# Routed experts of a decoder layer: blocks of two 64-row pieces in place of blocks of 128 rows

## The reference, cut to what matters

```python
x = x + attn(layernorm(x)); x = x + xattn(layernorm(x), ctx, ctx)
h0 = layernorm(x)                                   # 1024 tokens of 256
shared = (silu_and_mul(h0 @ shared_gate_up_w.T) @ shared_down_w.T) * sigmoid(h0 @ sgate_w.T)
routing_weights = softmax(h0 @ gate_w.T)            # 16 experts
topk_w, topk_ids = top_k(routing_weights, 4)
for e in range(16):                                 # w13[e]: 352 x 256, w2[e]: 256 x 176
    coef = sum(where(topk_ids == e, topk_w, 0.0), axis=-1)
    acc = acc + (silu_and_mul(h0 @ w13[e].T) @ w2[e].T) * coef[:, None]
out = x + shared + acc
```

## Time and profile before

| | us |
|---|---|
| median of 3 runs | 385.86 |
| lowest and highest run | 384.45 and 387.84 |
| the profiled execution, its own time | 389.97 |
| its span, from first to last instruction | 388.1 |

### The profile page before, as it was taken

One profiled execution on the slowest core, in us unless ns is written; L12 is line 12 of the kernel. 1 busy time (PEld: TensorE's weight loads), 2 busy tenths in 40 slices (PEclk: granted clock), 3 DMA queues, 4 the chain that ended last, 5 costly groups with the idle time before them and its releaser, 6 DMA issues.

```text
span 388.1 us, 7610 instructions
## 1 busy us (share of the span) xinstructions
PE 346.5 (89%) x2118; PEld 246.7 (64%) x2134; DVE 236.1 (61%) x730; ACT 182.4 (47%) x538; POOL 145.6 (38%) x179
## 2 busy tenths in 40 slices
PE   6988799999999998777869939999999999999883
PEld 2455376777666865556748626777777777778652
DVE  3296669898898499653445524444444444443995
ACT  1264579898878586735406213333333333332220
POOL 5491314362544140757157400333333333332000
PEclk9899799999999699885898979999999999999996
DMA  7997866778595814312112153677777777754901
GB/s 227 334 301 279 371 193 199 225 232 280 156 346 159 266 45 151 96 44 84 43 56 96 66 145 89 212 215 206 208 221 215 204 219 200 231 175 152 371 15 54
DMA packets 47365, 71.60 MB, mean 184 GB/s; under 512 B 5619, under 2 KB 35332, under 8 KB 46692
## 3 DMA queue, kind: packets, MB, share of 16 engines
q1 hardware_dynamic: 42692, 59.79, 50.2%
q0 software_dynamic: 3792, 10.49, 7.1%
q10 hardware_dynamic: 848, 0.92, 1.0%
HBM read 39.07 MB, written 32.12 MB: 183 GB/s over the span
## 4 chain that ended last, share of the span: by engine, by line
PE 32%; issue 25%; POOL 16%; DVE 14%; ACT 7%; DMA 3%; SPq 1%; POOLq 0%; DVEq 0%; ACTq 0%
POOL y_picks L605 11%; PE bank L1417 10%; ACT probs L641 6%; PE bank L1339 4%; PE bank L1295 3%; PE bank L1331 3%; DVE neg_max L881 2%; DVE x L1255 2%; POOL x_slots L551 2%; PE bank L1326 2%; PE bank L1387 2%; PE bank L1360 2%; PE bank L1400 1%; DVE probs_t L887 1%; PE bank L1368 1%
## 5 line engine op out<-in xcount | busy, mean ns | idle before, releaser
L605 POOL DMA_INDIRECT y_picks<-yb,ids x47 | 45.1, 960 | 85.9 <-DVE yb L1227 85.2
L641 ACT ACTIVATE probs<-bank,neg_max 128x128 f32<-128x128 f32 x256 | 70.1, 417 | 7.3 <-DVE neg_max L881 7.3
L1670 PE MATMUL bank<-w,xbt 128*128 x188 | 65.7, 474 | 0.6 <-ACT xbt L772 0.6
L1220 DVE TENSOR_TENSOR hb<-sg,bank 128x176 f32<-128x176 f32 x47 | 15.9, 339 | 60.2 <-ACT sg L780 53.4
L780 ACT ACTIVATE sg<-bank 128x176 f32<-128x176 f32 x47 | 14.9, 317 | 76.4 <-issue 56.8
L1690 PE MATMUL bank<-w,hbt 128*128 128x256 f32 x188 | 48.2, 380 | 0.0
L1670 PEld LDWEIGHTS bank<-w,xbt 128*128 128x128 f32 x188 | 32.9, 194 | 18.4 <-issue 2.5
L881 DVE TENSOR_REDUCE neg_max<-bank 128x4 f32<-128x512 f32 x64 | 41.4, 681 | 5.0 <-PE bank L1331 4.9
L1339 PE MATMUL bank<-ident,probs 128*128 128x128 f32 x256 | 40.1, 289 | 4.5 <-ACT probs L641 4.0
L551 POOL DMA_INDIRECT x_slots<-x,slots x32 | 32.2, 1006 | 28.0 <-DVE slots L1010 19.6
L1339 PEld LDWEIGHTS bank<-ident,probs 128*128 128x128 f32 x256 | 30.4, 147 | 11.3 <-ACT probs L641 10.9
(11 more groups left out here) (172 smaller groups left out, 668.5 us busy)
## 6 DMA issues: line engine op xcount, KB each, us to landing
x_slots<-zero_b SPq DMA_DIRECT2D x16, 1056.0 KB, 8.8
w<-w_in_dram SPq DMA_DIRECT2D x47, 256.0 KB
xb<-x_slots SPq DMA_DIRECT2D x47, 132.0 KB
w<-w_in_dram SPq DMA_DIRECT2D x4, 1408.0 KB, 11.6
yg<-y_picks SPq DMA_DIRECT2D x8, 512.0 KB, 7.0
ktc<-keys_d SPq DMA_DIRECT2D x16, 192.0 KB, 3.2
sw_raw<-shared_in_dram SPq DMA_DIRECT2D x6, 384.0 KB, 3.3
keys_d<-ctxt_h SPq DMA_DIRECT2D x4, 512.0 KB, 6.4
```

Of the source, the lines that this page charges most:

```text
L605: pool.indirect_dma_start(y_picks[:, :], bass.IndirectOffsetOnAxis(ids[:, n:n + 1], 0), yb[:, n % RB, :], None).then_inc(yb_placed[n % RB] ...
L641: ins = act.activation(probs[:, g, j, :], ps_s[g][:, 128 * j:128 * j + 128], ACT.Exp, bias=neg_max[:, g, j:j + 1])
L1670: ins = pe.matmul(ps_gu[n % 2][:, 0:GU], xbt[:, n % 2, k, :], w13[:, bass.ds(e, 1), k, :].rearrange("p e n -> p (e n)"), start=k == 0, sto ...
```

## The change

The blocks become pairs of 64-row pieces, the even and the odd piece each with its own expert: NBLK is 40 (79 pieces at most). The even piece has stationary columns and output rows 0 to 63, the odd one 64 to 127, in `block_up` and `block_down`. The even piece's weights are read by a register in place, `w13` and `w2`, of which now all 16 experts are in SBUF; the odd piece's up weights are copied by ScalarE into `w13_odd` (two buffers, `copy_up`), and its down weights are loaded by SyncE into `w2_odd` (a ring of RW = 3). The rows of a block no longer stand together, so GpSimd loads them by an indirect DMA with 128 row numbers (`gather_rows`). The table is made for both pieces.

```diff
-NBLK = (B * T * TOPK + NE * 127) // 128
+ROWS = 64
+NBLK = -(-((B * T * TOPK + NE * (ROWS - 1)) // ROWS) // 2)
+RW = 3
 RB = 4
...
+NEXP = WORDS * PACK
...
+        w13_odd = place("w13_odd", [128, 2, KC, GU])
+        w2_odd = place("w2_odd", [128, RW, KC, D])
...
-        w2 = place("w2", [128, RB, KC, D])
+        w2 = place("w2", [128, NE, KC, D])
...
             def load_down(n):
 
-                if n >= RB:
-                    sp.wait_ge(yb_psum, n - RB + 1)
+                if n >= RW:
+                    sp.wait_ge(yb_psum, n - RW + 1)
                 e = sp.value_load(table[0:1, n:n + 1], min_val=0, max_val=NE - 1)
...
+                sp.dma_start(w2_odd[:, n % RW, :, :].rearrange("p k d -> p (k d)"),
+                             w2_in[:, bass.ds(e, 1), :, :].rearrange("p e k d -> p (e k d)")).then_inc(w2_odd_loaded[n % RW], 16)
 
             sp.wait_ge(x3_ready, B)
+            for i in range(4):
+                es = slice(4 * i, 4 * i + 4)
+                sp.dma_start(w2[:, es, :, :], w2_in[:, es, :, :]).then_inc(w2_loaded, 16)
             sp.wait_ge(table_ready, 3)
-            for n in range(RB - 1):
+            for n in range(NBLK):
                 load_down(n)
-            sp.wait_ge(scattered, 16 * TOPK * B)
-            for n in range(RB + 1):
-                load_rows(n)
...
+            def gather_rows(n):
+
+                if n >= RB:
+                    pool.wait_ge(xbt_psum, n - RB + 1)
+                    pool.wait_ge(ids_ready, n - RB + 1)
+                pool.indirect_dma_start(xb[:, n % RB, :], None, x_slots[:, :],
+                                        bass.IndirectOffsetOnAxis(rows[:, n:n + 1], 0)).then_inc(xb_loaded[n % RB], 16)
+
+            pool.wait_ge(x3_ready, B)
+            pool.wait_ge(table_ready, 1)
+            pool.wait_ge(scattered, 16 * TOPK * B)
+            for n in range(RB):
+                gather_rows(n)
             for n in range(NBLK):
-                place_rows(n)
+                if n + RB < NBLK:
+                    gather_rows(n + RB)
+                if n:
+                    place_rows(n - 1)
+            place_rows(NBLK - 1)
...
+            act.wait_ge(table_ready, 2)
+            packed = [act.value_load(words[0:1, WORDS + i:WORDS + i + 1], min_val=0, max_val=NE ** PACK - 1) for i in range(WORDS)]
+            number = act.alloc_register("expert_odd")
+
+            def copy_up(n):
+
+                act.reg_alu(number, packed[n // PACK], 4 * (n % PACK), ALU.logical_shift_right)
+                act.reg_alu(number, number, NE - 1, ALU.bitwise_and)
+                e = act.snap(number, min_val=0, max_val=NE - 1)
+                if n >= 2:
+                    act.wait_ge(gu_psum, n - 1)
+                act.activation(w13_odd[:, n % 2, :, :], w13[:, bass.ds(e, 1), :, :].rearrange("p e k n -> p (e k) n"), ACT.Copy
+                               ).then_inc(w13_odd_ready, 1)
+
+            act.wait_ge(w13_loaded, 64)
+            act.wait_ge(x2_ready, B)
+            copy_up(0)
+            copy_up(1)
             take_rows_t(0)
             take_rows_t(1)
             block_gate(0)
+            copy_up(2)
             for n in range(NBLK):
                 if n + 1 < NBLK:
                     block_gate(n + 1)
                 take_hidden_t(n)
                 if n + 2 < NBLK:
                     take_rows_t(n + 2)
+                if n + 3 < NBLK:
+                    copy_up(n + 3)
...
             def block_table():
 
-                pe.wait_ge(after_ready, 1)
...
+                pe.wait_ge(after_ready, 2)
+                for part in range(2):
+                    at = TABLE_AT + NBLK * part
+                    for i in range(2):
+                        pe.matmul(ps_t[ROWS * i:ROWS * i + ROWS, at:at + NBLK], upto[:, NE:NE + ROWS],
+                                  after[:, part, i:2 * NBLK:2], start=True, stop=True)
+                at = TABLE_AT + 2 * NBLK
+                for i in range(2):
+                    ins = pe.matmul(ps_t[0:1, at + NEXP * i:at + NEXP * i + NEXP], upto[:, NE:NE + 1], after[:, 0, i::2],
+                                    start=True, stop=True)
+                ins.then_inc(table_psum, 1)
...
-                e = experts[n]
+                pe.wait_ge(w13_odd_ready, n + 1)
                 for k in range(KC):
-                    ins = pe.matmul(ps_gu[n % 2][:, 0:GU], xbt[:, n % 2, k, :],
-                                    w13[:, bass.ds(e, 1), k, :].rearrange("p e n -> p (e n)"), start=k == 0, stop=k == KC - 1)
+                    pe.matmul(ps_gu[n % 2][0:ROWS, 0:GU], xbt[:, n % 2, k, 0:ROWS],
+                              w13[:, bass.ds(experts[n], 1), k, :].rearrange("p e n -> p (e n)"), start=k == 0, stop=k == KC - 1)
+                    ins = pe.matmul(ps_gu[n % 2][ROWS:128, 0:GU], xbt[:, n % 2, k, ROWS:128], w13_odd[:, n % 2, k, :],
+                                    start=k == 0, stop=k == KC - 1)
...
                 for k in range(KC):
-                    ins = pe.matmul(ps_yb[n % 2][:, 0:D], hbt[:, n % 2, k, :], w2[:, n % RB, k, :], start=k == 0, stop=k == KC - 1)
+                    pe.matmul(ps_yb[n % 2][0:ROWS, 0:D], hbt[:, n % 2, k, 0:ROWS],
+                              w2[:, bass.ds(experts[n], 1), k, :].rearrange("p e n -> p (e n)"), start=k == 0, stop=k == KC - 1)
+                    ins = pe.matmul(ps_yb[n % 2][ROWS:128, 0:D], hbt[:, n % 2, k, ROWS:128], w2_odd[:, n % RW, k, :],
+                                    start=k == 0, stop=k == KC - 1)
```

More of the change, by code:

```diff
@@ L93, in decoder_layer @@
         tri = place("tri", [128, 2, 128], BF16)
-        upto = place("upto", [NE, NE + 128 + NBLK])
-        dump = place("dump", [128, NBLK])
+        upto = place("upto", [NE, NE + 128 + 2 * NEXP])
+        dump = place("dump", [128, 2 * NBLK + 1])
+        rows = place("rows", [128, NBLK], U32)
+        rows_f = place("rows_f", [128, NBLK])
         of_block = place("of_block", [128, NBLK])
@@ L131, in decoder_layer @@
         counts_i = place("counts_i", [NE, 2], I32)
-        after = place("after", [NE, NBLK])
-        table = place("table", [1, 2 * NBLK], I32)
-        words = place("words", [1, WORDS], I32)
+        after = place("after", [NE, 2, 2 * NEXP])
+        table = place("table", [1, NBLK], I32)
+        words = place("words", [1, 2 * WORDS], I32)
         ex = place("ex", [128, B, NE])
@@ L148, in decoder_layer @@
         cursor[0] = shared_at
[L149 to L153 removed]
+        packs = place("packs", [1, 2 * NEXP])
+        packed_f = place("packed_f", [1, 2 * NEXP])
+        words_f = place("words_f", [1, 2 * WORDS])
         cursor[0] = after_shared
@@ L353, in decoder_layer @@
         xb_loaded = [sem(f"xb_loaded{r}") for r in range(RB)]
-        w2_loaded = [sem(f"w2_loaded{r}") for r in range(RB)]
+        w2_loaded = sem("w2_loaded")
+        w2_odd_loaded = [sem(f"w2_odd_loaded{r}") for r in range(RW)]
+        w13_odd_ready = sem("w13_odd_ready")
         yb_placed = [sem(f"yb_placed{r}") for r in range(RB)]
@@ L1699, in _ @@
             pe.wait_ge(rows_added, HB)
+            pe.wait_ge(w2_loaded, 64)
             for n in range(NBLK):
```

70 lines of the change are left out of this document (25 added, 45 removed).

## The result

The changed kernel takes 375.73 us (median of 4 executions, 374.28 to 380.67) where the kernel before, run beside it, takes 386.85 us (384.45 to 388.37). The ratio is 0.9706, 95% interval 0.9631 to 0.978: faster. Ratios here leave out executions that are over 1.5% above the fastest of their kernel; medians don't. The profiled execution of the changed kernel took 375.47 us, with a span of 373.6, so it is like its median; the profiled one of before, 389.97, lay 3 us above the 386.85 here and 4 us above the 385.86 that the prediction started from.

A forecast was written before the change was run, and what follows sets the result against it. TensorE was taken to bound the block loop: 47 blocks at 2.50 us (117.5) become 40 at 2.80 (112.0), plus 0.4 at the start, 5.1 less. From the median 385.86 that gives 380.8 us, 8-in-10 range 375 to 394.

The forecast's parts named there:

- halves abreast at the price of one: Block loop on TensorE: two 64-column halves stream side by side, down 0.87 and up 1.19 us per block as now.
- rival 2: Halves don't overlap fully: period 3.32 us, time 402, chance 0.05; no overlap at all: 4.86 a block, 463, chance 0.02.
- the two switches together: TensorE, each block: changing between halves and full width adds 0.30 us (0.28 to 0.35), making the period 2.80.
- ScalarE's copy: Block loop: copying the odd piece's up weights on ScalarE takes 0.79 us, with 0.8 us cover, nothing on the path.
- rival 3: The path over xbt or the sequencer sets the period, 2.87 to 3.0 us: time 386, chance 0.15.
- rival 4: Switches hide, for instance behind waiting loads: period 2.50 to 2.60 us, time 371, chance 0.06.
- GpSimd's 2 x 1.27 = 2.54: Block loop: GpSimd's gather and scatter together take 2.54 of the 2.80 us period, fitting by 0.26.
- rival 1: GpSimd becomes the bound if a gather's span passes 1.22 us; at 1.6 the time is 396, chance 0.10.
- The forecast charged 0.4: Start of the block loop: word reads, table matmuls and slower first switches make 0.1 us; 0.4 taken because ScalarE stands close.
- The table's matmuls: Ahead of the loop on TensorE: two small matmuls taking 0.51 us become six with some two more switches, 0.5 us more.
- its like would take 384.9: Whole kernel: the profiled execution of 389.97 us less the 5.1 us forecast gain.
- the median of the runs is 4.1 lower: Whole kernel: median before is 385.86 us, 4.1 under the profiled execution; minus 5.1 gives 380.8.

The follow-up runs named there:

- run 6: Changed kernel with blocks taken two at a time on TensorE (two blocks' up passes, all their transposes, two blocks' down passes): 374.38 us, ratio 0.9755 to the kernel before.
- run 2: Changed kernel with up and down matmuls at full width, the even piece's expert for all 128 rows, odd experts left out: 370.07 us, ratio 0.9629.
- before with zeros at 42 us: Kernel before with six products of zeros on TensorE in the attention loop's wait near 42 us: 383.51 us, ratio 0.9996.
- run 4: Changed kernel with TensorE and ScalarE reading only the first word of experts ahead of the loop, the others in it: 380.17 us, ratio 0.986.
- changed with zeros at 42 us: Changed kernel with six products of zeros on TensorE in the attention loop's wait near 42 us: 378.31 us, ratio 0.9789.
- warm start: Changed kernel with products of zeros on TensorE behind each word it reads and behind the first transposes, ahead of the blocks: 379.09 us, ratio 0.9726.
- pairs and warm start: Changed kernel with blocks taken two at a time on TensorE and products of zeros ahead of the blocks: 378.92 us, ratio 0.9821.
- pairs, four buffers: Changed kernel with blocks taken two at a time and four rather than three buffers for the odd pieces' down weights: 376.73 us, ratio 0.977.
- all four: Changed kernel with blocks two at a time, four odd down-weight buffers, products of zeros ahead of the blocks and near 42 us: 376.06 us, ratio 0.9737.

## Why the prediction was right, and where it was off

*The forecast's own steps.* What it said of the loop held to one or two hundredths: halves abreast at the price of one (both forms of rival 2 fall, 402 and 463), period 2.785 for 2.80, the two switches together 0.285 for 0.30, 40 blocks at 2.785 = 111.4 for 112.0. That is 6.1 us less than 117.5 where 5.5 was worked out; from first up pass to last place the gain is 6.4. ScalarE's copy took 0.791 for 0.79; no path over `xbt` appeared (rival 3), TensorE was busy 20.00 of 20.00 us; the switches did not hide (rival 4), and run 6 takes one pair of them out and finds 0.30 us in the period. GpSimd's 2 x 1.27 = 2.54 left the 0.25 us that was forecast (rival 1), and run 2 shows the point from which it decides, 2.55 us a block.
By the Trainium skill, TensorEngine Tiling (Array Packing), Key Properties, a change of tiling mode drains TensorE. The trace agrees: 1.28 us for up passes that take 1.19 where no change follows, and 0.30 us less for one pair of switches less in run 6. By the Trainium skill, TensorE: Matmul & The Clock Gate, Part 3, The mechanism, matmuls are strictly in order in start and end. In this trace the odd half's first pass (281.77) starts ahead of the even half's second pass (282.06), which belongs to the instruction issued before it. So for fp32 matmuls in two passes the starts are not in order pass by pass; of the ends the trace can't tell, since they are modelled.

*The start of the loop.* The forecast charged 0.4. From the last scatter to the first up pass it was 10.7 us in three profiles of the changed kernel's start, and 9.7, 11.4 and 11.4 in three of the kernel before. The kernel with 47 blocks, whose eight words are as many as the kernel before reads, took 11.4 too. From the last x3 addition it is 34.4 to 34.5 with eight words (before, before with zeros at 42 us, 47 blocks) and 33.7 with seven (the changed kernel's three), and the clock's loss between explains at most 0.3 of that. So the start got about 0.6 us shorter, one word's price, and not 0.4 longer. The other terms were too high or fell on nothing. The table's matmuls cost 0.59 for 0.51 us, not 0.5 more. The chain of the changed kernel there:

```profile
212.51 2.87 DMA x_slots<-x,slots
...
216.19 3.60 DMA xb<-x_slots,rows
219.79 2.15 issue
221.94 0.68 PE bank L1700 x2
...
222.64 0.39 ACT xbt L782
...
223.18 0.84 PE bank L1710
```

A gather's rows are there 3.6 us after its start and not 2.5, which no one waited for, since TensorE reads its seven words from 216.5 to past 220.6 (4.1 us for six steps, 0.68 each, 0.69 forecast); run 4 took the reads away and ran into the gather.

*The step that failed* is the one before the sum's end: "its like would take 384.9" and "the median of the runs is 4.1 lower, 385.86; minus 5.1 is 380.8". It takes for granted that all that lies ahead of the blocks stays as it is, and that one offset carries both kernels from a profiled execution to their median. The code there stayed; its time did not. Of 11.1 us between the medians first measured, the loop explains 6.4. In the profiles the rest lies ahead of the blocks, where TensorE's clock falls in one profile and not in another in code that the change leaves alone. The last column is the clock's loss from the start to the last scatter:

| profile of | clock 42 to 50 us | clock 124 to 136 us | first up pass | loop | last scatter | clock's loss ahead of it |
|---|---|---|---|---|---|---|
| before | 0.60 | 0.72 | 231.3 | 121.2 | 221.5 | 18.8 |
| before, again | 0.60 | 0.86 | 231.8 | 121.0 | 220.4 | 18.8 |
| before with zeros at 42 us | 1.00 | 0.72 | 230.1 | 121.1 | 218.8 | 17.1 |
| changed | 1.00 | 1.00 | 223.2 | 114.8 | 212.5 | 10.2 |
| changed, again | 0.79 | 1.00 | 225.1 | 115.1 | 214.5 | 11.9 |
| changed with zeros at 42 us | 1.00 | 1.00 | 224.9 | 114.8 | 214.2 | 10.2 |
| in pairs | 1.00 | 1.00 | 222.0 | 112.8 | 211.3 | 8.5 |
| full width | 0.59 | 0.86 | 226.4 | 105.2 | 215.7 | 13.7 |
| 47 blocks | 0.79 | 0.86 | 229.7 | 134.3 | 218.3 | 15.4 |
| words read late | 0.62 | 0.86 | 229.8 | 115.6 | 220.3 | 18.8 |
| warm start | 0.58 | 0.72 | 230.1 | 113.0 | 219.5 | 18.8 |
| pairs and warm start | 0.60 | 0.86 | 230.4 | 111.8 | 219.9 | 18.8 |
| pairs, four buffers | 0.57 | 0.72 | 230.2 | 111.5 | 219.5 | 18.8 |
| all four | 1.00 | 0.72 | 228.2 | 109.9 | 217.6 | 15.4 |

The loop's length goes with what each form does to the loop. The first up pass goes with the clock, though not with the two stretches alone: full width and the kernel before, once more, are alike there (0.59 and 0.60, 0.86) and 5.4 us apart. Taken as a whole it does: the last scatter lies at 211.3 to 221.5 us, and less the clock's loss ahead of it at 200.7 to 204.0 in all fourteen, 201.6 to 202.8 in the kernel before and 202.3 to 204.0 in the changed one. Between the first two profiles the last scatter differs by 9.0 us, and the loss by 8.5.

It is not a matter of the change as such: seven of the eleven profiles of the changed kernel and its forms lose the clock near 128 us as the kernel before does, and six of these at 42 us too (the one with 47 blocks, at 0.79, in part). With this the account of the change closes. Over all executions the kernel before has a median of 386.2 us (72 of them) and the changed one, unedited, 377.5 (10): 8.7 less, and 8.9 in the mean spans. Of these 6.4 are the loop's, 0.6 the start's, and up to 2.0 the clock's. Against the forecast of 5.1 less, the loop gave 0.9 more, the start 1.0 more, and the clock up to 2.0. The 2.4 us by which the first result (375.73 beside 386.85) exceeds this are luck of few executions. The gain of loop and start alone, 7.0, taken off 386.85, would give 379.9, 0.9 under the forecast: so far its mechanism bears it. That 375.73 still lies inside the range, by 0.7 us, is not its merit.

**Still open** is whether the 2.0 us are chance. One execution's loss scatters by 2.7 us (standard deviation) about its mean, and only ten of the changed kernel are unedited; with the zeros at 42 us the two kernels lose the same. Four of the fourteen profiles kept the clock near 128 us: both of the changed kernel, the one with the zeros at 42 us and that of the pairs. Nothing was found in the code that sets this.

## What to carry to other kernels

A tile of half the columns costs nothing on TensorE as long as its partner streams beside it: count moving columns, add 0.28 to 0.30 us for each pair of switches between tiled and untiled work, and put work of one shape together so that there are few such pairs. Before a stage is blamed or praised for a difference of two profiles, compare the same instructions' times ahead of it and the granted clock there, and take (1 - clock) x time off both; here 8.1 of the 14.5 us between the first two profiles came ahead of the stage that was changed. And an engine with a fixed price per operation, as GpSimd with 1.27 us for each indirect DMA, gives the floor of the loop: 2.55 us here, 0.23 under the period.

## What the runs showed of the hardware

The clock fell in a stretch in which TensorE had work without a gap. In the kernel before, in order of time:

```profile
127.10 0.39 PE L1417 MATMUL bank<-gate_h,xth 128*128 128x18 f32 x2
...
128.46 0.37 PE L1417 MATMUL bank<-gate_h,xth 128*128 128x18 f32 x2
128.69 0.41 PE L1417 MATMUL bank<-gate_l,xth 128*128 128x18 f32 x2
128.95 0.58 PE L1417 MATMUL bank<-gate_h,xtl 128*128 128x18 f32 x2
```

These are the gate's products, of 18 columns each; two passes take 0.37 us, and from 128.95 on 0.58. In five of the fourteen profiles the clock fell amid these products (clock 0.72 from 124 to 136 us), in five in the products by `wqkv` right behind them (0.86), and in four not at all; in the changed kernel's profile the same products run through at 0.37. What a fall costs can be read off the additions: the changed kernel is 3.3 us ahead at the first x3 addition and 6.6 at the fifth, so 3.3 each for these two.

Ahead of the fall near 44 us TensorE had been idle for 1.33 us. Idle time alone does not decide it: the wait was the same 1.32 to 1.34 us in all eleven profiles without products of zeros there, and the clock fell in nine of them and kept its level in two (the changed kernel and the pairs). With six products of zeros in the wait it kept its level in three of three.
